# A transformer block on one core: the second LayerNorm's result modulated by ScalarE's copy, the router's moments taken on TensorE, b1's order from one mask, and the last steps in another order

## The chip, the cores and the metric

The kernel runs on one core of one Trainium2 chip. A core has five engines that work side by side, each on its own queue of instructions: PE (TensorE, matmuls), DVE (VectorE), ACT (ScalarE), POOL (GpSimd) and SP (SyncE, here only DMA issues). The metric is the device time of one execution in microseconds (us); less is better. A change of more than 2% is called faster or slower.

## The reference

Eight sequences of 256 tokens with 128 features go through causal attention with 16 heads of 8 and through a mixture of eight experts, both under adaptive LayerNorm:

```python
mod = (_silu(L0_c) @ L0_wmod).reshape(8, 6, 1, -1)
sa, ca, ga, sb, cb, gb = (mod[:, i] for i in range(6))   # ga, gb: magnitude at least 0.25
h = _layernorm(x) * (1 + ca) + sa
x = x + ga * attention(h, W_qkv, W_o)        # causal, ALiBi slopes
h = _layernorm(x) * (1 + cb) + sb
x = x + gb * ffn(h, W1, b1, W2, b2, ln_gamma, ln_beta, Wr, br)

# ffn: its input goes to the experts as it is; the router sees a LayerNorm of it
hr = (h - mu) * rsqrt(var + 1e-5) * ln_gamma + ln_beta
probs = softmax(hr @ Wr + br)                # 8 experts
# expert 0 has W1, b1, W2, b2; experts 1 to 7 all have the same perturbed copies
out = sum_e probs[e] * (gelu(h @ W1[e] + b1[e]) @ W2[e] + b2[e])
# perturbed copy: w * 0.2 for the largest 5% of |w|, w * 1.8 for the smallest 5%
```

Since experts 1 to 7 are equal, the kernel computes two experts and weighs the second with the sum of seven probabilities. The thresholds of the perturbation are found for W1 and W2 by a search over 31 bits, and for the short vectors b1 and b2 by rank: for each element, how many are larger and how many are smaller.

## The kernel before, in words

The order of every engine's instructions is written out by hand. After a prologue comes a loop over steps `t` = 0 to 39 on all engines, four steps per batch (`G` = 4 groups of 4 heads), and after it a last stage that is written line by line.

In step `t`, `s_unit` makes scores whose maxima DVE takes (L1204, L1208, into `nmax`); five steps later `e_unit` makes the same scores again with the maxima subtracted, ACT takes the exponential (L584, into `PT`), POOL applies the causal mask (L494), and `pv` (L819, L824) multiplies with the values. `ut` (L837) transposes the result `U`, which ACT has copied out (L694); after every second group DVE normalizes it into `A` (`rden` L1415, `A` L1419). At offset `AT_OT` = 10 of a batch `A` is transposed (L1020) and copied (`AT`, L590), at `AT_Y` = 11 it is projected with the gated output weight (L1027), and DVE adds it to `x_all` (L1425). Through step 31 each step also carries a bit of the threshold search: ACT and DVE count over `wa` (L599, L1183), PE sums the counts (`total`, L930, L932), DVE decides.

Then the second half of the block begins for that batch. `second_stats` (DVE, L1227, L1230) takes its moments, `second_rstd` (POOL, L437, L439) the inverse deviation, `second_normal` (POOL, L451) writes `n2`. `second_use` (DVE, L1239, two instructions) multiplies `n2` by 1 + cb and adds sb, with rows that DMAs have broadcast to all partitions (`rows_bc`), into `h2`. `router_stats` (DVE, L1249, L1252) takes the moments of `h2` for the router's LayerNorm. For each pair of batches `p`, `c_pe_h` (PE, L858) transposes `h2`, `c_act_h` (ACT, L607) copies it out as `h2T`, and `c_pe_l` (PE, L865) multiplies it with `wrg` (Wr scaled by gamma) for the logits. `router_logits` (DVE, L1261 to L1270), `c_exp` (POOL, L460, a power of e) and `router_weights` (DVE, L1275 to L1287) make the weights of the two experts. `f1(n)` and `f2(n)` (PE, L898 and L918) are the two layers of pair `n // 2`, of expert 0 for even and of the perturbed expert for odd `n`; `f1_ahead` (L881) does the first layer for `n` = 0 and 2 in steps 26 to 34. `combine(n)` (DVE, L1302; for odd `n` also L1309, L1315) adds the result of `f2(n)`.

`psX`, the last bank of PSUM, serves many in turn. Whoever writes to it next calls `claim_x(reader)`: PE first waits until the last reader named has read, and the queue behind it on PE waits too.

For b1's ranks POOL makes eight masks (`bias_masks`, L475, one in each of steps 8, 9, 12, 13, 16, 17, 18 and 20: b1 larger and b1 smaller than a column of 128 of its elements, four columns), PE sums them with a vector of ones (L1052, in steps 21 to 26), and DVE makes the perturbed b1 in step 27 (`perturb_b1`, L1335 to L1339). For b2 the masks are made by DVE in step 23 (L1354), summed in step 31 (L1044), and used in step 32. `find_tiers` and `perturb` (L1324 to L1331) do the same for W1 in steps 33 and 34, and for W2 in steps 38 and 39.

Of the kernel before, what the change touches and what calls it, by code (L numbers as in the profile page):

```python
# [23 lines left out]
P = 128  # L24
# [4 lines left out]
NC = FF // P  # L29
# [21 lines left out]
SIGNS_STEP, VEC_STEP, ROWS_STEP, SIZE_STEP, BIAS_STEP, WO_STEP = 0, 0, 1, 7, 31, 7  # L51
ROW_DMAS = 4
# [3 lines left out]
AT_STAT2, AT_STAT3 = AT_Y, AT_Y + 3  # L56
# [3 lines left out]
H2_AT = {AT_Y + G * b + 2 + (b >= LATE): b for b in range(B - 1)}  # L60
RSTD3_AT = {22: 0, 30: 1, 38: 2}
# [15 lines left out]
POOL_SETS = 9  # L77
# [8 lines left out]
def adaln_block(nc, x, w_qkv, w_o, w1, b1, w2, b2, gamma, beta, wr, br, c, wmod,  # L86
                k_const, q_const, ident_c, parts_dram, rows_dram, thr_dram, out):
    with ExitStack() as ctx:
# [3 lines left out]
        def sem(name):  # L92
# [26 lines left out]
        wrg = sb("wrg", [P, NE])  # L119
# [6 lines left out]
        rows_bc = sb("rows_bc", [P, B, 4, D])  # L126
# [30 lines left out]
        n2 = sb("n2", [P, 4, D])  # L157
        h2 = sb("h2", [P, NPAIR, 4, D])
        h2T = sb("h2T", [P, 2, 4 * P])
        mv3 = sb("mv3", [P, B * NBLK, 2])  # L160
        ve3 = sb("ve3", [P, B * NBLK])
        rs3 = sb("rs3", [P, B * NBLK])
        lgT = sb("lgT", [NE, 4 * P])
# [13 lines left out]
        rmask = hid.rearrange("p a c t -> p (a c t)").bitcast(BF16).rearrange("p (m k c t) -> p m k c t", m=2, k=2, c=NC)[:, 1]  # L177
# [8 lines left out]
        rows = lgT.rearrange("e (r d) -> e r d", r=4)  # L186
# [13 lines left out]
                 "ln_stat", "ln_rstd", "neg_mean", "n1_done", "t_done", "h1_done", "qk_done", "v_done", "v_out",  # L200
# [4 lines left out]
                 "tot_done", "cond_done", "ln2_stat", "ln2_rstd", "n2_done", "h2_done", "gate_in", "ln3_stat", "ln3_rstd",  # L205
# [6 lines left out]
        rows_in = [sem(f"rows_in{i}") for i in range(ROW_DMAS)]  # L212
# [36 lines left out]
        def _(sp):  # L249
# [11 lines left out]
            block_in(1)  # L261
            sp.dma_start(wa[0:HALF, :], w1.rearrange("(p r) f -> p (r f)", r=2)).then_inc(q["wa_in"], 16)
# [14 lines left out]
            def rows_to_dram():  # L277

                sp.wait_ge(q["dve_set"], SETS["rows"])
                sp.wait_ge(q["act_set"], ACT_SETS["cg"])  # L280
                sp.dma_start(rows_dram, rows[:, :, :]).then_inc(q["rows_out"], 16)
# [5 lines left out]
            def other_rows(i):  # L287
                bs = slice(i * B // ROW_DMAS, (i + 1) * B // ROW_DMAS)
                for b in range(bs.start, bs.stop):
                    sp.dma_start(rows_bc[:, b, 1:4, :], rows_dram[b, 1:4, :].partition_broadcast(P)).then_inc(rows_in[i], 16)  # L290
# [60 lines left out]
            other_rows(0)  # L351
# [6 lines left out]
            other_rows(1)  # L358
            sp.dma_start(w1_sb[:, :], w1).then_inc(q["w1_in"], 16)
            sp.dma_start(w2_sb[:, :, :], w2.rearrange("(c p) d -> p c d", p=P)).then_inc(q["w2_in"], 16)  # L360
            for b in range(4, B):
# [3 lines left out]
                if b < 6:  # L365
                    other_rows(b - 2)
# [17 lines left out]
        def _(gp):  # L384
# [4 lines left out]
            for i in range(3):  # L389
                gp.memset(Vx[:, i], 1.0).then_inc(q["pool_set"], 1)  # L390
            gp.memset(beta_w[:, :], 1.0).then_inc(q["pool_set"], 1)

# [32 lines left out]
            def gate(b):  # L425

                if b == 0:
                    gp.wait_ge(q["pe_set"], 7)
# [15 lines left out]
            def second_normal(b):  # L444

                gp.wait_ge(q["ln2_rstd"], b + 1)
                if b >= 2:
                    gp.wait_ge(q["h2_done"], b - 1)
                for i in range(NBLK):
                    k = NBLK * b + i  # L450
                    last = gp.tensor_scalar(n2[:, NBLK * (b % 2) + i, :], x_all[:, b, i, :], mv1[:, k, 0:1], rs1[:, k:k + 1],  # L451
# [3 lines left out]
            def router_ln(p):  # L455
                deviation("ln3_stat", (2 * p, 2 * p + 1), ve3, mv3, rs3, "ln3_rstd")
# [1061 lines left out]
```

## Time and profile before

| | us |
|---|---|
| median of 3 runs | 238.66 |
| the three runs | 238.48, 238.66, 248.0 |
| the profiled execution's own time | 239.84 |
| its span in the trace | 238.1 |

The profiled execution is a run of its own, with 239.84 us of which the trace covers 238.1; the 1.7 us around it lie before the first and after the last instruction. Times in the trace are counted from the start of the span. In the trace's windows, steps 0 to 31 run from about 18 to 158 us, steps 32 to 39 to about 185 us, and the last stage to the end.

### The profile page before, as it was taken

To read this page: it belongs to the slowest core of one execution; us is meant where nothing else is said; L and a number is where in the kernel's file an instruction comes from. 1 tells how busy PE (TensorE), PEld (TensorE's weight loads), DVE (VectorE), ACT (ScalarE), POOL (GpSimd) and SP (SyncE) were. 2 spreads that over 40 slices of the span, in tenths; PEclk is the share of its full clock that TensorE was granted. 3 is DMA by queue.
4 is the path that set the end of the run, shared out by engine and by line. 5 is a ranking of instruction groups with operands and counts; after the bars stand their busy time and mean duration, and the time that the engine had idled before them with its cause. 6 is when DMAs were issued, how large, how long until landed. Compare 5 with 4: busy or idle time off the path is not lost.

```text
span 238.1 us, 5477 instructions
## 1 busy us (share of the span) xinstructions
PE 216.5 (91%) x1901; PEld 152.5 (64%) x1918; DVE 185.0 (78%) x562; ACT 162.6 (68%) x344; POOL 143.6 (60%) x223
## 2 busy tenths in 40 slices
PE   8977989899899899889879879979879999999993
PEld 3554757676676676666667556735535878766793
DVE  4767899889799899998998876974967585675464
ACT  2577658989989989979669769937628741453320
POOL 8650232758979979988666236437779608283600
PEclk9997999999999999999999999999985999999999
DMA  6668665965948137237036000000000001010011
GB/s 179 118 185 224 153 168 140 243 183 143 249 120 211 41 95 213 53 96 194 6 89 181 26 0 6 0 0 6 3 0 3 0 3 44 0 45 3 0 44 44
DMA packets 19461, 20.90 MB, mean 88 GB/s; under 512 B 1547, under 2 KB 17562, under 8 KB 18370
## 3 DMA queue, kind: packets, MB, share of 16 engines
q1 hardware_dynamic: 18746, 20.22, 32.5%
q10 hardware_dynamic: 688, 0.33, 0.5%
q8 instruction: 15, 0.25, 0.4%
q14 instruction: 12, 0.10, 0.2%
HBM read 15.16 MB, written 5.26 MB: 86 GB/s over the span
## 4 chain that ended last, share of the span: by engine, by line
PE 63%; DVE 18%; ACT 7%; issue 7%; POOL 4%; ACTq 0%; DVEq 0%; POOLq 0%
PE bank L918 12%; PE bank L898 10%; PE bank L819 6%; DVE nmax L1208 4%; PE bank L715 4%; PE bank L776 4%; ACT msk L599 3%; PE bank L798 3%; PE bank L881 3%; PE bank L772 3%; PE bank L952 3%; PE bank L824 2%; DVE msk L1183 2%; PE bank L932 2%; PE bank L930 2%
## 5 line engine op out<-in xcount | busy, mean ns | idle before, releaser
L494 POOL TENSOR_SCALAR_AFFINE_SELECT PT<-PT 128x256 f32<-128x256 f32 (+1 forms) x96 | 46.8, 502 | 35.0 <-ACT PT L584 32.8
L599 ACT ACTIVATE msk<-wa,cand 128x1024 bf16<-128x1024 f32 (+1 forms) x62 | 57.7, 941 | 5.3 <-DVE cand L1194 5.3
L584 ACT ACTIVATE PT<-bank 128x512 f32<-128x512 f32 x96 | 55.5, 607 | 5.0 <-PE bank L793 3.4
L1208 DVE TENSOR_REDUCE nmax<-bank 128x2 f32<-128x512 f32 x64 | 43.5, 685 | 2.5 <-PE bank L776 1.8
L460 POOL TENSOR_TENSOR ex<-eul,lg 128x32 f32<-128x32 f32 x4 | 21.7, 5436 | 17.2 <-DVE lg L1270 17.2
L1204 DVE TENSOR_REDUCE nmax<-bank 128x4 f32<-128x512 f32 x32 | 21.7, 677 | 4.3 <-PE bank L769 4.2
L776 PE MATMUL bank<-Ks,Qs 78*128 78x256 bf16 x128 | 24.8, 276 | 0.0
L798 PE MATMUL bank<-Qs,Ks 80*128 80x256 bf16 x128 | 24.5, 273 | 0.2 <-ACT PT L584 0.2
L1183 DVE TENSOR_SCALAR_CACHE_REDUCE msk<-wa,cand 128x512 bf16<-128x512 f32 x31 | 23.1, 746 | 1.1
L819 PE MATMUL bank<-PT,Vx 128*32 128x256 f32 x256 | 20.9, 398 | 1.6 <-POOL PT L494 1.0
L772 PE MATMUL bank<-mask 128*128 128x256 bf16 x64 | 18.0, 281 | 2.9 <-DVE nmax L1208 2.4
L694 ACT ACTIVATE U<-bank 128x256 f32<-128x256 f32 x32 | 12.7, 398 | 11.5 <-PE bank L824 11.4
L624 ACT ACTIVATE hid<-bank,b1p 128x512 f32<-128x512 f32 x16 | 10.7, 687 | 10.6 <-PE bank L898 10.6
L1302 DVE SCALAR_TENSOR_TENSOR yt<-bank,pr,yt 128x128 f32<-128x128 f32 x32 | 9.1, 345 | 10.6 <-PE bank L918 10.5
L715 PE MATMUL bank<-ones_b 128*128 128x512 bf16 x49 | 16.3, 454 | 1.0 <-POOL ones_b L385 1.0
L898 PE MATMUL bank<-h2T,w1p 128*128 128x512 f32 x32 | 16.8, 656 | 0.0
L918 PEld LDWEIGHTS bank<-w2p,hid 128*128 128x128 f32 x128 | 14.8, 192 | 1.4 <-issue 1.4
L837 PE MATMUL bank<-ident,U 128*128 128x128 f32 x64 | 13.4, 292 | 1.7 <-DVE A L1419 1.0
L918 PE MATMUL bank<-w2p,hid 128*128 128x128 f32 x128 | 14.9, 275 | 0.0
L769 PE MATMUL bank<-Ks,Qs 78*128 78x128 bf16 x128 | 12.4, 218 | 1.9 <-DMA Ks<-parts 0.9
L776 PEld LDWEIGHTS bank<-Ks,Qs 78*128 78x128 bf16 x128 | 12.8, 100 | 1.8 <-issue 0.3
L769 PEld LDWEIGHTS bank<-Ks,Qs 78*128 78x128 bf16 x128 | 9.9, 97 | 5.8 <-issue 1.3
(196 smaller groups left out, 489.6 us busy)
## 6 DMA issues: line engine op xcount, KB each, us to landing
Qs<-parts SPq DMA_DIRECT2D x7, 576.0 KB
Ks<-parts SPq DMA_DIRECT2D x7, 576.0 KB
parts<-part SPq DMA_DIRECT2D x7, 384.0 KB, 2.8
rows_bc<-rows_out SPq DMA_DIRECT2D x8, 192.0 KB, 7.9
x_all<-in_x SPq DMA_DIRECT2D x8, 128.0 KB, 7.0
parts<-part SPq DMA_DIRECT2D x8, 128.0 KB, 2.9
out<-ob SPq DMA_DIRECT2D x3, 256.0 KB, 2.3
wa<-in_w SPq DMA_DIRECT2D x2, 256.0 KB, 4.6
```

What stands on the lines that cost most here:

```text
L494: gp.affine_select(out=v, in_=v, compare_op=ALU.is_ge, fill=0.0, base=0, pattern=[[0, v.shape[1]], [1, P]], channel_multiplier=-1).then_in ...
L584: act.activation(PT[:, e % 2, j], psE[u % 2][:, :], ACT.Exp).then_inc(q["exp_done"], 1)
L599: act.activation(scratch, wa[:, 0:width], ACT.Sign, bias=cand[:, col:col + 1].bitcast(F32), scale=-(1.0 - 2.0 ** -24), accum_out=acc[:, co ...
L715: mm(psU.rearrange("p (a k) -> p a k", a=HG), ones_b[:, :], ones4, start=True, stop=True)
L772: mm(bank.rearrange("p (h k) -> p h k", h=2)[:, :, P:S], mask5[:, HG, :], mask5[:, 0:2, :], start=True, stop=False, skip_group_check=True)
L776: last = mm(bank[:, i * S:(i + 1) * S], Qs[0:R_S, r, h, P:S], Ks[0:R_S, r, h, :], start=False, stop=True, skip_group_check=True)
L798: last = mm(bank[:, i * S:(i + 1) * S], Ks[0:R_E, r, h, 0:P], Qs[0:R_E, r, h, :], start=True, stop=True, skip_group_check=True)
L819: mm(psO[32 * i:32 * i + 32, 0:S], Vx[:, b % 4, 0, h, :], PT[:, e % 2, 1 + i // 2, (i % 2) * S:(i % 2 + 1) * S], start=True, stop=False, s ...
L898: mm(psF[ch][:, :], wt[:, ch * P:(ch + 1) * P], h2T[:, p % 2], start=True, stop=True).then_inc(q["f1_done"], 1)
L918: last = mm(bank[:, i * P:(i + 1) * P], hid_of(n)[:, ch, i * P:(i + 1) * P], wt[:, ch, :], start=(ch == 0), stop=(ch == NC - 1), skip_grou ...
L1183: ve.tensor_scalar(msk[:, 3], wa[:, ON_ACT:2 * FF], cand[:, BOT:BOT + 1].bitcast(F32), 0.0, op0=ALU.is_le, op1=ALU.add, accum_out=acc_d[:, ...
L1208: ve.tensor_reduce(nmax[:, b % 2, 1, h:h + 2], bank.rearrange("p (h k) -> p h k", h=2), axis=AX.X, op=ALU.max, negate=True).then_inc(q["ma ...
```

## The change

The second modulation (1 + cb, sb) leaves DVE and the DMAs: `n2` itself is transposed, so that a feature is a partition, and ACT's copy out of PSUM multiplies and adds with one column per batch (`mod2T`), in two instructions of half the size. `second_use`, `router_stats` and the broadcasts of the two modulation rows go; of the four rows per batch only ga's and gb's are still broadcast, gb's by one DMA behind the loads of batch 7. `mod2T` comes from two small matmuls in the prologue.

The router's moments now come from PE: `wrg` has a ninth column with 1/128, so that the logits' matmul yields the mean too; DVE squares `h2T` (`squares`), and four more matmuls yield the mean of the squares.

```diff
             def c_pe_l(p):
-                pe.wait_ge(q["h2T_done"], p + 1)
+                pe.wait_ge(q["h2T_done"], 2 * (p + 1))
                 claim_x((q["lg_read"], p + 1))
                 for i in range(4):
-                    last = mm(psX[:, i * NE:(i + 1) * NE], h2T[:, p % 2, i * P:(i + 1) * P], wrg[:, :], start=True, stop=True)
+                    last = mm(psX[:, i * (NE + 1):(i + 1) * (NE + 1)], h2T[:, p % 2, i * P:(i + 1) * P], wrg[:, :], start=True, stop=True)
                 last.then_inc(q["lg_psum"], 1)
+                pe.wait_ge(q["sq_done"], p + 1)
+                for i in range(4):
+                    last = mm(psX[:, MSQ_COLS + i:MSQ_COLS + i + 1], sq[:, i * P:(i + 1) * P], wrg[:, NE:NE + 1], start=True, stop=True)
+                last.then_inc(q["sq_sum"], 1)
...
+            def squares(p):
+                v.wait_ge(q["h2T_done"], 2 * (p + 1))
+                if p:
+                    v.wait_ge(q["sq_sum"], p)
+                ve.tensor_tensor(sq[:, :], h2T[:, p % 2], h2T[:, p % 2], op=ALU.mult).then_inc(q["sq_done"], 1)
...
+            def router_moments(p):
+                raw = psX[:, 0:4 * (NE + 1)].rearrange("p (i e) -> p i e", i=4)
+                v.wait_ge(q["sq_sum"], p + 1)
+                then_self(ve.tensor_copy(mean3[:, :], raw[:, :, NE]))
+                ve.tensor_tensor(msq3[:, :], mean3[:, :], mean3[:, :], op=ALU.mult)
+                then_self(ve.tensor_tensor(lt[:, :, :], e8(mean3[:, :]), g8(gsum[:, 0:NE]), op=ALU.mult))
+                ve.scalar_tensor_tensor(ve3[:, 4 * p:4 * p + 4], psX[:, MSQ_COLS:MSQ_COLS + 4], EPS, msq3[:, :], op0=ALU.add,
+                                        op1=ALU.subtract).then_inc(q["ln3_var"], 1)
+                ve.tensor_tensor(lg[:, :, :], raw[:, :, 0:NE], lt[:, :, :], op=ALU.subtract).then_inc(q["lg_read"], 1)
...
                 combine(n)
                 p = n // 2 + 1
-                if p < NPAIR:
-                    (router_weights if n % 2 else router_logits)(p)
+                if p < NPAIR and n % 2 == 0:
+                    squares(p)
+                    router_moments(p)
+                    router_logits(p)
+                elif p < NPAIR:
+                    router_weights(p)
```

For pair 0 the squares are made in step 32, `c_pe_l(0)` stands at the end of step 33 (before: step 36), the moments in step 34.

For b1 there is one mask per column instead of two: DVE makes all four at the end of step 31, and the instruction's own accumulator gives the count of larger elements the other way; PE sums them at the end of step 32 (16 matmuls instead of 32), `perturb_b1` stands in step 33. b2's masks are made in step 7.

```diff
-B1_AT, B1_USE = (8, 9, 12, 13, 16, 17, 18, 20), 27
-B1_RANKS = {21: (0,), 22: (1,), 23: (2, 3), 24: (4,), 25: (5,), 26: (6, 7)}
...
+            def bias_masks():
+                v.wait_ge(q["b1abs_done"], 1)
+                for i in range(NC):
+                    last = ve.tensor_scalar(rmask[:, i], b1a[:, :], colsa[:, i:i + 1], 0.0, op0=ALU.is_gt, op1=ALU.add,
+                                            accum_out=b1_over[:, i:i + 1])
+                last.then_inc(q["b1m_done"], 1)
...
+                if t == BIAS_STEP + 1:
+                    pe.wait_ge(q["b1m_done"], 1)
+                    claim_x((q["b1p_done"], 1))
```

The remaining edits move work. In the prologue `w_o` is loaded by SP instead of ACT's queue and its transpose follows `projected(0)`, with one spare matmul ahead of that instead of two; the variance plus epsilon of batch 0 is made by DVE; in step 0 the second scores and two spare matmuls stand ahead of `total`. In steps 36 to 39 the four parts of `f1(1)` stand ahead of `ut` instead of at the end of the step, and in step 32 `f1_ahead` stands ahead of `pv`. DVE adds to `x_all` ahead of `rden` and `A`. POOL's `router_ln` takes its variance from `router_moments`.

On PE, the start of the last stage of before (w_sb are the plain weights, w2p and w1p the perturbed ones):

```order
L1027 MATMUL bank<-woTg,AT 128x128 x2
L898 MATMUL bank<-h2T,w1p 128x512
L918 MATMUL bank<-w_sb,Qs 128x128 x16
L865 MATMUL bank<-wrg,h2T 128x8 x4
L898 MATMUL bank<-h2T,w1p 128x512 x4
L918 MATMUL bank<-w2p,hid 128x128 x16
```

and the same place of the changed kernel:

```order
L891 MATMUL bank<-h2T,w1p 128x512
L1032 MATMUL bank<-woTg,AT 128x128 x2
L911 MATMUL bank<-w_sb,Qs 128x128 x16
L854 MATMUL bank<-wrg,h2T 128x9 x4
L858 MATMUL bank<-wrg,sq 128x1 x4
L891 MATMUL bank<-h2T,w1p 128x512 x4
L911 MATMUL bank<-w2p,hid 128x128 x16
```

The four matmuls on `sq` are new, between the logits of pair 1 and `f1(3)`; the same stands twice more, for pairs 2 and 3.

On DVE, from `x_all` of batch 5 (step 31) to the first part of `find_tiers` of W1 (step 33), before:

```order
L1425 TENSOR_TENSOR x_all<-x_all,bank 128x256
L1227 BN_STATS st<-x_all 128x6 x2
L1230 BN_AGGR mv<-st 128x2 x2
L1389 COPY Ks<-bank 128x512
L1335 TENSOR_SCALAR b2t<-bank 128x128
...
L1389 COPY Ks<-bank 128x512
L1415 RECIPROCAL rden<-bank 128x16
L1419 TENSOR_TENSOR A<-bank,rden 128x2x64
L1097 TENSOR_SCALAR w1p<-w_sb 128x512
```

and in the changed kernel:

```order
L1416 TENSOR_TENSOR x_all<-x_all,bank 128x256
...
L1226 BN_STATS st<-x_all 128x6 x2
L1229 BN_AGGR mv<-st 128x2 x2
L1343 TENSOR_SCALAR hid,b1_over<-b_bc,colsa 128x512 x4
L1391 COPY Ks<-bank 128x512
L1327 TENSOR_SCALAR b2t<-bank 128x128
...
L1237 TENSOR_TENSOR sq<-h2T 128x512
L1391 COPY Ks<-bank 128x512
L1327 TENSOR_SCALAR rtmp<-b1_over 128x4
...
L1422 RECIPROCAL rden<-bank 128x16
L1426 TENSOR_TENSOR A<-bank,rden 128x2x64
L1097 TENSOR_SCALAR w1p<-w_sb 128x512
```

The four masks (L1343), the squares (L1237) and the five instructions of the perturbed b1 (from L1327 on) have come in.

## Rows read from the trace of the kernel before

**Rows 1.** The page: each engine's busy time, and TensorE's granted clock in 40 slices.

```profile
PE 216.5 (91%) x1901; PEld 152.5 (64%) x1918; DVE 185.0 (78%) x562; ACT 162.6 (68%) x344; POOL 143.6 (60%) x223
PEclk9997999999999999999999999999985999999999
```

**Rows 2.** Busy time of each engine by window (start:end, length, busy us, clock).

```profile
62.00:97.00 35.00, 32.60 (x358) 23.36 (x361) 32.30 (x97) 32.48 (x74) 31.59 (x55) 1.00 0.56 151
97.00:132.00 35.00, 31.37 (x372) 23.01 (x375) 31.67 (x89) 29.70 (x68) 25.54 (x43) 1.00 0.38 101
157.90:174.40 16.50, 13.77 (x145) 7.71 (x145) 12.34 (x31) 10.28 (x22) 10.64 (x19) 1.00 0.01 3
185.00:200.00 15.00, 15.00 (x114) 13.09 (x113) 10.61 (x36) 7.07 (x12) 7.56 (x6) 1.00 0.00 1
```

**Rows 3.** The chain that ended last, last stage (start, length, what).

```profile
189.28 3.54 PE bank L898 x8
192.82 3.57 PE bank L918 x32
...
200.40 0.79 PE bank L865 x8
```

**Rows 4.** Groups of instructions by line and shape (busy us, mean ns).

```profile
L475 POOL TENSOR_SCALAR hid<-b_bc,colsa 128x512 bf16<-128x512 f32 x8 | 12.6, 1574 | 0.0
L1239 DVE TENSOR_TENSOR h<-n,rows_bc 128x256 f32<-128x256 f32 x8 | 3.9, 483 | 2.3 <-POOL n L451 2.3
L1239 DVE TENSOR_TENSOR h<-h,rows_bc 128x256 f32<-128x256 f32 x8 | 3.6, 446 | 0.3
L1249 DVE BATCH_NORM_STATS2 st<-h 128x6 f32<-128x128 f32 x16 | 3.8, 282 | 0.1
L541 ACT ACTIVATE h1T<-bank,modT 128x256 f32<-128x256 f32 x8 | 4.5, 564 | 4.3 <-PE bank L942 4.3
L1052 PE MATMUL bank<-ones_b,hid 128*128 128x1 bf16 x32 | 1.6, 163 | 2.6 <-DVE x_all L1425 1.3 <-ACT AT L590 1.3
L1183 DVE TENSOR_SCALAR_CACHE_REDUCE msk<-wa,cand 128x512 bf16<-128x512 f32 x31 | 23.1, 746 | 1.1
L439 POOL TENSOR_TENSOR rs<-ve,mhalf 128x4 f32<-128x4 f32 x4 | 4.2, 1040 | 0.3
L1267 DVE TENSOR_TENSOR lg<-lg,rs 128x32 f32<-128x32 f32 x4 | 0.8, 192 | 0.1
```

**Rows 5.** The chain that ended last, steps 13 and 14.

```profile
72.37 1.56 POOL hid L475
...
78.83 0.92 POOL hid L475
```

**Rows 6.** Waits: who waited for whom, total, times, longest.

```profile
PE bank L1027 <- DVE b1p L1339: 1.2, 1, 1.2
```

**Rows 7.** Prologue: two spare matmuls ahead of the first projection; the window at 20 us.

```profile
7.00 1.06 PE L715 MATMUL bank<-ones_b 128*128 128x512 bf16 x2
20.00:21.00 1.00, 1.00 (x5) 0.39 (x4) 0.86 (x3) 0.97 (x3) 0.00 (x0) 0.50 0.94 274
```

**Rows 8.** Instructions in order of time, steps 31 to 37.

```profile
157.93 0.41 DVE L1425 TENSOR_TENSOR x_all<-x_all,bank 128x256 f32<-128x256 f32 x1
...
174.41 0.41 DVE L1425 TENSOR_TENSOR x_all<-x_all,bank 128x256 f32<-128x256 f32 x1
174.64 0.41 PE L837 MATMUL bank<-ident,U 128*128 128x128 f32 x2 [1.00 <-DVE A L1419]
...
178.46 5.44 POOL L460 TENSOR_TENSOR ex<-eul,lg 128x32 f32<-128x32 f32 x1
```

**Rows 9.** Instructions of DVE in order of time, last stage.

```profile
193.42 1.12 DVE L1302 SCALAR_TENSOR_TENSOR yt<-bank,pr,yt 128x128 f32<-128x128 f32 x4
...
201.46 0.19 DVE L1275 TENSOR_REDUCE esum<-ex 128x4 f32<-128x32 f32 x1 [2.38 <-POOL ex L460]
...
203.58 0.69 DVE L1287 TENSOR_TENSOR yt<-yt 128x512 f32<-128x512 f32 x1
```

More of the change, by code:

```diff
@@ L285, in gate_rows, with last_rows @@
                 sp.dma_start(rows_bc[:, :, 0, :], rows_dram[:, 0, :].partition_broadcast(P)).then_inc(q["gate_in"], 16)
[L287 to L290, printed above, removed]
+            def last_rows():
+                sp.dma_start(rows_bc[:, :, 1, :], rows_dram[:, 1, :].partition_broadcast(P)).then_inc(q["gb_in"], 16)
             def write_first():
@@ L606, in c_act_h @@
                     act.wait_ge(q["lg_psum"], p - 1)
-                act.activation(h2T[:, p % 2], (psE[1] if p >= 2 else psQ)[:, :], ACT.Copy).then_inc(q["h2T_done"], 1)
+                    act.wait_ge(q["sq_done"], p - 1)
+                for k in range(2):
+                    b = 2 * p + k
+                    act.activation(h2T[:, p % 2, S * k:S * (k + 1)], (psE[1] if p >= 2 else psQ)[:, S * k:S * (k + 1)], ACT.Identity,
+                                   scale=mod2T[:, 1, b:b + 1], bias=mod2T[:, 0, b:b + 1]).then_inc(q["h2T_done"], 1)
             def gelus(n, chunks=range(NC)):
@@ L974, in _ @@
             mm(psE[1][0:B, 0:512], c_s[:, :], wmod_sb[:, 2 * D:6 * D], start=True, stop=True).then_inc(q["pe_set"], 1)
+            pe.wait_ge(q["dve_set"], SETS["modT"])
+            for j in range(2):
+                last = mm(psE[0][:, j * B:(j + 1) * B], wmod_sb[:, (3 + j) * D:(4 + j) * D], c_s[:, :], start=True, stop=True)
+            last.then_inc(q["pe_set"], 1)
             turned(1)
@@ L1004, in _ @@
                     total(n)
+                if first and t in AHEAD and t >= B * G:
+                    f1_ahead(*AHEAD[t])
                 pv(t)
@@ L1011, in _ @@
                 e_unit(t, 2)
-                if t in AHEAD and t >= B * G:
+                if t in AHEAD and t >= B * G and not first:
                     f1_ahead(*AHEAD[t])
+                if t in F1_STEPS:
+                    f1(1, F1_STEPS[t])
                 ut(t)
@@ L1039, in _ @@
                     router_sums()
+                if t == BIAS_STEP + 1:
+                    pe.wait_ge(q["b1m_done"], 1)
+                    claim_x((q["b1p_done"], 1))
+                    for m in range(NC):
+                        for j in range(NC):
+                            last = mm(psX[:, B1_COLS + m:B1_COLS + m + 1], rmask[:, j, m * P:(m + 1) * P], ones_b[:, 0:1],
+                                      start=(j == 0), stop=(j == NC - 1), skip_group_check=True)
+                    last.then_inc(q["b1rank"], 1)
+                if t in H_STEP:
+                    c_pe_h(H_STEP.index(t))
+                if t in AHEAD and t < B * G:
+                    f1_ahead(*AHEAD[t])
                 if t == BIAS_STEP:
@@ L1429, in _ @@
                     second_stats(b)
-                if t in H2_AT:
-                    second_use(H2_AT[t])
-                b = batch_at(t, AT_STAT3)
-                if b is not None:
-                    router_stats(b)
                 if t == SIGNS_STEP:
@@ L1455, in _ @@
                     perturb_b2()
-            second_use(B - 1)
-            router_stats(B - 1)
+                if t == SQUARE_STEP:
+                    squares(0)
+                if t == MOMENT_STEP:
+                    router_moments(0)
             router_weights(0)
```

204 lines of the change are left out of this document (81 added, 123 removed).

## The prediction

> **What bounds the kernel now.** I read the page first. TensorE is busy for 216.5 of 238.1 us, the others for 60 to 78% [rows 1]; but a busy share is an average, so the stages are read one by one. The windows of the loop [rows 2] show that no engine rules there: from 62 to 132 us (70 us) ACT is busy for 32.48 + 29.70 = 62.2 us, DVE for 64.0, PE for 64.0, POOL for 57.1. Whoever is late in a step holds up the next one, so work taken from one engine gives back only a part. In the last stage it is another picture: PE is busy for 15.00 of 15.00 us [rows 2], and the chain of waits there runs over PE alone, eight blocks of `f2` (3.57 us) and five of `f1` (3.54) with the logits' 0.79 between [rows 3]. DVE has slack there, but what PE waits for in that stage moves the end one for one. Between the two, in steps 31 to 39, DVE is busy for 12.34 of 16.50 us [rows 2], and its chain decides when PE may go on (1.00 us of waiting for `A` at 174.64) [rows 8]. Clock: TensorE's granted clock is at its full level (2.4 GHz) but for two dips to half of it (1.2 GHz), in slice 4 and in slices 30 and 31 of the page [rows 1].
>
> **The change part by part. Loop.** DVE loses `second_use` and `router_stats`: 3.9 + 3.6 + 3.8 = 11.3 us over eight batches [rows 4], 1.4 each and some small aggregates, four of them in the 70 us. POOL loses eight masks, 12.6 us [rows 4], in steps 8 to 20; two of them stand on the chain for 1.56 + 0.92 = 2.5 us [rows 5]. PE loses 16 of 32 rank matmuls, and two places where its whole queue stood behind them: 1.3 us behind `x_all` [rows 4], 1.2 us behind the perturbed b1 [rows 6]. If the 70 us shrank to what PE and ACT have to do (62.4, with 0.8 us less on PE and a bit of cleared waiting), 7.6 would be won. Today 6 of 70 us are lost although three engines are close to full; with DVE relieved I leave 4 of them, so 66.3 and a gain of 3.7. With b1's 1.2, which lies behind 132 us, the loop gives 4.9. Bounds: 2.5 (only the stretch on POOL's chain) and 9.5 (7.6, b1's wait, and the same rate for the steps to 158 us).
>
> **Prologue.** One of two spare matmuls ahead of the first projection goes: half of 1.06 us at most [rows 7], I take 0.4. Putting the second scores of step 0 ahead of `total` fills PE's wait there. At 20 us the clock was at half [rows 7]; if it stays up, 1 to 2 us of PE's time are saved, of which DVE, busy for 0.86 us in that window, lets through about half: 1.0. The DMA of `w_o`, now in SP's queue ahead of `wa`, can take some of it back. Together 1.4, bounds 0 and 2.4. The two small matmuls for `mod2T` stand beside PE's wait for ACT; ACT's two copies replace two others.
>
> **Steps 31 to 37.** DVE gets four masks, 4 x 0.746 less their overlap = 2.8 us (the same instruction, a compare with an accumulator over 512 columns, is the threshold count) [rows 4]; `squares(0)`, 0.69 as any two-input instruction of 128x512 [rows 9]; five small instructions for b1, about 1.0; the moments, five at 0.19 [rows 4], 0.95. It loses one `second_use` and `router_stats`, about 2.2 here. Net 3.3: from 12.34 to 15.6 of 16.5 us [rows 2]. That would just fit if it never waited, but now it does. At the end of step 32 PE must claim `psX` behind `perturb_b2`, which on DVE has moved behind the masks (2.8 us later), and in step 34 the transpose of `A` claims the same bank behind `router_moments(0)`, which stands behind `find_tiers` and `perturb`. I followed both queues from `x_all` of batch 5 (157.93 us): the moments end at 174.2, PE then does step 35 (1.9 us) and the projection, and `x_all` of batch 6 ends at 177.0 instead of 174.41 + 0.41 = 174.8 [rows 8]. So +2.2 us; bounds 0 and +4. Moving `f1(1)` ahead of `ut` saves PE some 4 us up to `f2(0)`, but the next paragraph shows why nobody gets them.
>
> **Last stage.** Behind `f2(0)` PE does the logits of pair 1 and now waits for `squares(1)`, which DVE does after `combine(0)`, which waits for `router_weights(0)`, which waits for POOL's power for pair 0. Before, that power ended at 178.46 + 5.44 = 183.90, 9.1 us after `x_all` of batch 6 [rows 8], and nobody on PE cared. Now: 177.0 + 9.1 = 186.1; router weights 203.58 + 0.69 - 201.46 = 2.8 [rows 9]; `combine` 1.12 [rows 9] and `squares` 0.69, with gaps 1.85; four more matmuls, which cost what the logits' four cost, 0.79 [rows 3]. `f1(3)` starts at 191.65 instead of 189.28 [rows 3]: +2.4, which holds the +2.2 above.
> From there to `f1(4)` it took 201.19 - 189.28 = 11.9 us [rows 3]. Now, from the start of `f1(3)`: moments 0.95, the inverse deviation 1.04 [rows 4] (before it was long done), logits 0.9, power 5.44, all with gaps: 8.4. `combine(1)` begins at 3.54 + 3.57 = 7.1 and takes 2.65, `router_weights(1)` to 12.6, `combine(2)` and `squares(2)` to 14.5, the four matmuls to 15.3. +3.4. For pair 3 the same sum gives 17.1 against 15.3: there PE has one `f1` more in between and only its own wait counts. +1.8. The sum of the stage is 2.4 + 3.4 + 1.8 = 7.6 us. The least it can cost is one time 1.85 per pair (the wait for `combine` and `squares`, of which the logits hide 0.79, and 0.79 for the new matmuls): 5.6, if DVE is never late. ACT's copy `h2T` in two instructions costs 2 x 0.564 [rows 4], some 0.5 us more per pair, beside a whole `f2`.
>
> **Sum.** 7.6 - 4.9 - 1.4 = +1.3 us on the span of 238.1 and on the profiled execution's 239.84. The median of the runs is 238.66, 1.2 us under that execution, so 238.66 + 1.3 = 240.0 us.
>
> **Rivals.** *The stalls bring the clock down.* In each of the three places PE now does 0.79 us of matmuls of 9 columns, stands still for 1 to 2.6 us and does 0.79 us with one column. The two dips of before came behind the same picture: the second began about 2 us after PE had waited 1.00 us for `A` at 174.64 [rows 8], with the logits of pair 0 in between, and covers some 6.5 us of slices 30 and 31 [rows 1]. In 6.5 us at half the clock 3.3 us are lost. It decides from the point where the first stall is answered by a clock of 0.5 in `f1(3)`: one dip gives 243.3, three give 249.9. For it: the picture. Against it: PE waited 1.3 us at one blow in the loop [rows 4], and no dip followed. The Trainium skill, TensorE: Matmul & The Clock Gate, Part 1, says that the rate follows how busy the array was lately and has just these two levels, which is this rival; the rows agree that it falls behind poorly filled stretches, and do not tell whether these are poor enough. Chance 0.22.
> *The removed work was not on the chain.* DVE's modulation does not appear in the chain of waits of the loop; if only POOL's 2.5 us come back and the prologue gives nothing, 238.66 + 7.6 - 2.5 = 243.8. Chance 0.17.
> *The loop gives much more.* 9.5 and 2.4 from the upper bounds, and steps 31 to 37 cost nothing: 5.6 - 11.9 = -6.3, 232.4. For it: with three engines near full, relief of two may loosen more than I leave. Chance 0.16.
> My forecast holds 0.45.
>
> **The numbers.** 2% of 238.66 is 4.8 us, about what a measurement here can tell from no change; so faster is below 233.9, slower above 243.4. Faster: most of the third rival (0.11) and a tail of the forecast (0.03), 0.14. Slower: of the clock's what is more than one dip (0.14), half of the second's (0.09), and a tail of the forecast (0.05), 0.28. Same: 0.58. The range reaches from 234.0 (into the third rival) to 247.0 (one or two dips).
>
> **What would show it.** In the changed kernel's chain of waits: three stalls of PE between the two groups of small matmuls, ended by DVE's `sq`, 2 to 3 us from the end of each `f2` to the next `f1`; a distance from the start of `f1(3)` to `f1(4)` of 15.3 us. In step 34 a PE wait before the transpose of `A` that DVE's `lg` ends. Steps of the loop (spacing of the first `nmax`) shorter by 0.1 to 0.2 us from step 8 on. A clock of 1.0 at 20 us. If the loop shrinks by over 8 us, or if `squares` is ready before PE asks, the forecast is too high; a half clock in the last stage makes it too low.

## The result and the profile after

The changed kernel takes 250.24 us (median of four runs, 247.39 to 251.96), the kernel before 239.13 us in the runs beside it: ratio 1.043, 95% interval 1.031 to 1.055. It is 11 us slower, where +1.3 was forecast, and lies outside the range. In a later round on another chip, the same file gave 250.21 us and 1.042 (1.035 to 1.048). Single executions of a kernel can take some per cent longer at a lower granted clock and are left out of the ratios; the profiled execution of the changed kernel (251.96 us, 1.7 us over its median) is one of these, so what is read from it is set beside other traces further down.

The page of the changed kernel, busy times and two lines of its slices:

```profile
span 250.2 us, 5459 instructions
...
PE 224.8 (90%) x1922; PEld 159.1 (64%) x1938; DVE 177.3 (71%) x539; ACT 163.8 (65%) x348; POOL 129.5 (52%) x211
...
PE   7779989899999999999999999699985987998993
...
PEclk9995999999999999999999999657998897999999
```

Against before [rows 1], DVE is busy for 7.7 us less, POOL for 14.1 less, ACT for about as long (163.8 us against 162.6), and PE for longer (224.8 against 216.5). The clock line says why: there is half clock in slice 4, in 26 to 28, in 31 and 32, and in 34. Places in the two traces, set against each other, say what each stretch cost. The stretches are cut at `x_all` of batches 5 and 6 and at the starts of `f1` as the chain of waits has them (192.04 us for `f1`(3), 0.14 us behind the start in the timeline below):

| stretch | before | after | difference | predicted |
|---|---|---|---|---|
| start to step 1 (first `nmax`) | 24.34 | 25.87 | +1.5 | -1.4 |
| step 1 to `x_all`(5) | 133.59 | 126.72 | -6.9 | -4.9 |
| `x_all`(5) to `x_all`(6) | 16.48 | 22.81 | +6.3 | +2.2 |
| `x_all`(6) to `f1`(3) | 14.87 | 16.64 | +1.8 | +0.2 |
| `f1`(3) to `f1`(4) | 11.91 | 17.28 | +5.4 | +3.4 |
| `f1`(4) to `f1`(6) | 15.3 | 19.32 | +4.0 | +1.8 |
| `f1`(6) to the end | 21.6 | 21.6 | 0 | 0 |
| sum | | | +12.1 | +1.3 |

The sum is that of the spans, 250.2 against 238.1.

The timeline of PE after, behind step 31 (start, duration, line, operation; in brackets PE's idle time ahead of it and who ended it):

```profile
155.86 0.39 PE L787 MATMUL bank<-Qs,Ks 80*128 80x256 bf16 x2
156.43 0.44 PE L826 MATMUL bank<-ident,U 128*128 128x128 f32 x2 [0.18 <-ACT U L683]
159.06 0.56 PE L1051 MATMUL bank<-ones_b,hid 128*128 128x1 bf16 x16 [2.19 <-DVE b2p_bc L1331]
...
170.47 1.84 PE L874 MATMUL bank<-h2T,w_sb 128*128 128x512 f32 x2
172.14 0.38 PE L826 MATMUL bank<-ident,U 128*128 128x128 f32 x2
172.36 0.38 PE L1025 MATMUL bank<-ident,A 128*128 128x128 f32 x2
```

And in the last stage:

```profile
187.43 0.96 PE L854 MATMUL bank<-wrg,h2T 128*128 128x9 f32 x8
190.99 1.05 PE L858 MATMUL bank<-wrg,sq 128*128 128x1 f32 x8 [2.60 <-DVE sq L1237]
191.90 5.38 PE L891 MATMUL bank<-h2T,w1p 128*128 128x512 f32 x8
...
208.27 1.05 PE L858 MATMUL bank<-wrg,sq 128*128 128x1 f32 x8 [2.61 <-DVE sq L1237]
209.18 5.38 PE L891 MATMUL bank<-h2T,w_sb 128*128 128x512 f32 x8
...
227.59 1.05 PE L858 MATMUL bank<-wrg,sq 128*128 128x1 f32 x8 [1.22 <-DVE sq L1237]
228.50 3.68 PE L891 MATMUL bank<-h2T,w_sb 128*128 128x512 f32 x8
```

The windows of the same stretches (busy time of each engine, then the granted clock, DMA share and GB/s):

```profile
157.00:159.00 2.00, 0.00 (x0) 0.00 (x0) 1.86 (x7) 0.00 (x0) 1.30 (x3) 0.86 0.00 0
159.00:172.00 13.00, 12.94 (x86) 8.24 (x87) 7.66 (x21) 4.14 (x8) 4.69 (x8) 0.50 0.01 2
190.00:192.00 2.00, 1.01 (x9) 1.01 (x10) 0.90 (x2) 0.00 (x0) 0.00 (x0) 1.00 0.00 0
192.00:196.00 4.00, 4.00 (x7) 1.72 (x7) 1.45 (x9) 1.37 (x2) 2.13 (x2) 0.57 0.00 0
209.00:213.00 4.00, 4.00 (x8) 1.81 (x9) 1.45 (x9) 1.15 (x2) 1.86 (x2) 0.58 0.00 0
```

Read them together. PE stands still for 2.19 us at the end of step 32 because DVE has not finished b2; from the last 0.6 us of that wait on it has half its clock (1.2 GHz), for 13.6 us in all, and from 159 to 172 us it is busy for 12.94 of 13.00 us. `f1`(3) and `f1`(4), each behind a wait of 2.6 us for the squares, show 5.38 us for eight rows that take 3.68 at `f1`(6), behind a wait of only 1.22. The forecast's own rows are all there: the three waits ended by `sq`, in the right places. What was not there is the wait ahead of `A`'s transpose in step 34 (172.36): at half clock PE comes to that place later than DVE.

One correction to the section on the change: b2's masks and the absolute values of b1 and b2 stand in step 30, not in step 7 (DVE makes the masks at 149.41). It changes no term of the sum.

### The profile page after: what moved, and what is told of

Same layout as the page of the kernel before. It is cut to its first block, busy times and chain, and to the rows that moved or that the text cites. A ratio compares the mean times of both kernels' runs of the same rounds, so it can differ in the third digit from the quotient of the medians.

```text
span 250.2 us, 5459 instructions
## 1 busy us (share of the span) xinstructions
PE 224.8 (90%) x1922; PEld 159.1 (64%) x1938; DVE 177.3 (71%) x539; ACT 163.8 (65%) x348; POOL 129.5 (52%) x211
## 4 chain that ended last, share of the span: by engine, by line
PE 55%; DVE 23%; issue 5%; ACT 5%; DMA 5%; POOL 3%; SPq 1%; DVEq 0%; ACTq 0%
PE bank L911 9%; PE bank L891 8%; PE bank L808 5%; DVE nmax L1207 5%; PE bank L765 3%; PE bank L787 3%; DVE msk L1182 3%; PE bank L874 3%; PE bank L761 3%; PE bank L704 2%; PE bank L923 2%; POOL ex L453 2%; PE bank L813 2%; DMA wa<-in_w 2%; PE bank L945 2%
## 5 line engine op out<-in xcount | busy, mean ns | idle before, releaser
L787 PE MATMUL bank<-Qs,Ks 80*128 80x256 bf16 x128 | 25.5, 281 | 0.6 <-ACT PT L569 0.6
L1203 DVE TENSOR_REDUCE nmax<-bank 128x4 f32<-128x512 f32 x32 | 21.6, 676 | 5.1 <-PE bank L758 5.1
L449 POOL TENSOR_TENSOR rs<-ve,mhalf 128x4 f32<-128x4 f32 x4 | 4.1, 1020 | 24.7 <-DVE ve L1249 24.7
L613 ACT ACTIVATE hid<-bank,cols 128x512 f32<-128x512 f32 x8 | 5.5, 687 | 17.1 <-PE bank L891 17.1
L761 PEld LDWEIGHTS bank<-mask 128*128 128x128 bf16 x64 | 7.7, 120 | 10.3 <-DVE nmax L1207 6.4
```

What stands on the lines that cost most here:

```text
L761: mm(bank.rearrange("p (h k) -> p h k", h=2)[:, :, P:S], mask5[:, HG, :], mask5[:, 0:2, :], start=True, stop=False, skip_group_check=True)
L787: last = mm(bank[:, i * S:(i + 1) * S], Ks[0:R_E, r, h, 0:P], Qs[0:R_E, r, h, :], start=True, stop=True, skip_group_check=True)
```

## The experiments

Theory C (clock): the long waits for DVE are the cause, but most of the loss comes from the clock that falls behind them. Rival W (waits alone): the waits and the new matmuls themselves cost the time. Theory M: DVE's four masks in step 31 make the wait of step 32. Theory P: the prologue's edit costs time. Theories C and M, with the wait as the cause and the clock behind it, can both hold. Runs of different groups ran on different chips, so their ratios to the kernel before are what is compared.

**First group.** The changed kernel once more:

> The changed kernel itself, on the same chip as the three edits sent with it, so that they can be set against it. All theories: about 250 us, 1.04 times the kernel before, a PE wait of about 2.2 us ahead of b1's rank matmuls in step 32 and half clock behind it until about 172 us, and PE waits of 2.6, 2.6 and 1.2 us for the squares in the last stage.

Measured: 250.21 us, ratio 1.042 (1.035 to 1.048).

*Spare matmuls in the waits*, in `c_pe_l` and in step 32 (`fill(bank, k)` makes k matmuls of 512 columns that nobody reads):

```diff
                 last.then_inc(q["lg_psum"], 1)
+                if p:
+                    fill(psE[1], 12)
                 pe.wait_ge(q["sq_done"], p + 1)
...
                     pe.wait_ge(q["b1m_done"], 1)
+                    pe.wait_ge(q["max_done"], 3 * G * B)
+                    fill(psS[1], 10)
                     claim_x((q["b1p_done"], 1))
```

> The changed kernel plus spare matmuls (nothing reads them) in the four places where PE waits for DVE: 10 ahead of b1's rank matmuls in step 32, 12 between the logits and the squares' sums of pairs 1, 2 and 3. The waits for DVE stay as long as they are, only PE isn't idle in them. Clock theory (the idle stretches themselves cost little, the granted clock that falls behind them costs about 3.7 us in steps 32 to 34 and 1.7 us each at f1(3) and f1(4)): 7 us faster than the changed kernel, about 243 us, granted clock 1.0 from 155 us on. Waits-alone theory (the extra time is the waits and the added small matmuls, the clock is only beside it): no faster than the changed kernel, 250 to 252 us, since nothing is taken from the path and pair 3's 12 spare matmuls overrun its wait by about 1.3 us.

Measured: 244.28 us, 1.022 (1.016 to 1.027). Work that nobody reads made the kernel 6 us faster than it was on the same chip (250.21); C holds and W alone falls. Its clock line, whose one low digit is slice 4:

```profile
PEclk9997999999999999999999999999999999999999
```

PE's timeline at the same place as above:

```profile
181.33 0.96 PE L858 MATMUL bank<-wrg,h2T 128*128 128x9 f32 x8
182.14 2.75 PE L708 MATMUL bank<-ones_b 128*128 128x512 bf16 x12
184.88 1.05 PE L864 MATMUL bank<-wrg,sq 128*128 128x1 f32 x8
185.79 3.68 PE L897 MATMUL bank<-h2T,w1p 128*128 128x512 f32 x8
```

`f1`(3) follows the logits' end as late as before, yet takes 3.68 us. This run also prices the waits without the clock: `x_all`(5) to `x_all`(6) 18.60 us (150.70 to 169.30), against 22.81, so 4.2 us of that stretch were clock; `f1`(3) to `f1`(4) 15.59, against 17.28, 1.7 us. Pair 3's spare matmuls overrun their wait: `f1`(4) to `f1`(6) is 18.74 us (201.38 to 220.12), where the changed kernel's 19.32 less the 1.70 us of half clock in `f1`(4) is 17.6. These 1.1 us are about what the result lies above the expected 243.

*b1's ranks in a bank of their own.*

```diff
                 elif ch < 3:
                     pe.wait_ge(q["max_done"], 3 * G * B)
+                    if ch == 2:
+                        pe.wait_ge(q["b1p_done"], 1)
...
-                    claim_x((q["b1p_done"], 1))
+                    pe.wait_ge(q["max_done"], 3 * G * B)
...
-                            last = mm(psX[:, B1_COLS + m:B1_COLS + m + 1], rmask[:, j, m * P:(m + 1) * P], ones_b[:, 0:1],
+                            last = mm(psS[1][:, m:m + 1], rmask[:, j, m * P:(m + 1) * P], ones_b[:, 0:1],
```

The first of these edits is in `f1_ahead`: its third part writes to the bank that the ranks now use, and so has to wait until DVE has read them.

> The changed kernel with b1's ranks in a PSUM bank of their own (the one of the score maxima, free by then), so that they needn't wait for DVE's b2 arithmetic: the wait of 2.2 us in step 32 has no reason left, the last stage is as it was. Clock theory: 2.2 us of wait and about 3.7 us of half clock go, 244 to 245 us, clock 1.0 through steps 32 to 34. Waits-alone theory: 2.2 us go, about 248 us. A third possibility, that the half clock there has another cause (the 16 one-column rank matmuls): it stays low behind them, and about 2 us go.

Measured: 252.55 us, 1.056 (1.050 to 1.061), slower than the changed kernel: a miss of all three. PE's timeline of it:

```profile
154.26 0.55 PE L1053 MATMUL bank<-ones_b,hid 128*128 128x1 bf16 x16
...
156.00 0.39 PE L787 MATMUL bank<-Qs,Ks 80*128 80x256 bf16 x2
...
159.09 1.74 PE L876 MATMUL bank<-h2T,w_sb 128*128 128x512 f32 x2 [2.70 <-DVE b1p L1333]
```

The rank matmuls don't wait any more, and the clock is 1.00 on them and until 158 us: these 16 matmuls of one column didn't bring it down. But the score bank that they now use is needed by the next `f1_ahead`, which waits for the perturbed b1, and that lies 2.3 us further down DVE's queue than b2 (done at 158.9 us, b2 at 156.6). The wait was moved and got longer (2.70 us), and the half clock came with it. `x_all`(5) to `x_all`(6) is 22.50 us (149.99 to 172.49), against 22.81: nothing is gained there. That the kernel got slower still comes from the last stage, whose code is unchanged. There the square sums ahead of `f1`(3) take 1.86 us instead of 1.05, and `f1`(6) is at half clock too, a third dip:

```profile
226.56 5.38 PE L893 MATMUL bank<-h2T,w_sb 128*128 128x512 f32 x8
```

So giving the ranks another bank doesn't help as long as DVE's queue is what they wait for, which points to theory M.

*The squares earlier.*

```diff
+            squares(1)
             router_weights(0)
             for n in range(2 * NPAIR):
+                if n == 4:
+                    squares(3)
                 combine(n)
                 p = n // 2 + 1
+                if n == 1:
+                    squares(2)
                 if p < NPAIR and n % 2 == 0:
-                    squares(p)
```

> The changed kernel with DVE's squares of pairs 1, 2 and 3 ahead of router_weights(0), router_weights(1) and combine(4), so that PE's square sums follow its logits at once. Step 32 stays. Clock theory: 2.6 + 2.6 + 1.2 us of waits and 2 x 1.7 us of half clock in f1(3) and f1(4) go, 9.8 us, about 240.5 us. Waits-alone theory: 6.4 us, about 244 us. If the squares push combine or router_weights back by their 0.7 us each and PE then waits there: 242 to 243 us.

Measured: 239.65 us, 0.996 (0.991 to 1.001): 10.6 us less than the changed kernel on the same chip, where C expected 9.8 and W 6.4. The clock line:

```profile
PEclk9955699999999999999999999985599999999999
```

PE's timeline:

```profile
191.08 0.96 PE L854 MATMUL bank<-wrg,h2T 128*128 128x9 f32 x8
191.89 1.03 PE L858 MATMUL bank<-wrg,sq 128*128 128x1 f32 x8
192.78 3.68 PE L891 MATMUL bank<-h2T,w1p 128*128 128x512 f32 x8
...
203.88 0.96 PE L854 MATMUL bank<-wrg,h2T 128*128 128x9 f32 x8
```

1.9 us of small matmuls in a row, but no wait: no dip in the last stage. The dip of step 32 (slices 27 to 29) is still there, and so is its wait (2.20 us). The one in slices 3 to 5 is taken up at the end. `f1`(3) to `f1`(4) is 12.81 us (192.78 to 205.59), 0.9 over the kernel before; that is the price of the four new matmuls, for which 0.79 was counted.

**Second group.** *The masks one per step*, with the absolute values of b1 and b2 in step 26:

```diff
-                if t == BIAS_STEP:
-                    bias_masks()
+                if 0 <= t - 27 < NC:
+                    bias_mask(t - 27)
```

> The changed kernel with b1's four masks one each in steps 27 to 30 (the absolutes in step 26) instead of all four in step 31, so that DVE's b2 arithmetic comes 2.7 us earlier and PE's claim of psX in step 32 finds it done. The last stage is as it was. Theory: DVE's backlog of masks makes the stall in step 32, and the stall the half clock. Stall and half clock go (2.2 + 3.7 us); the masks cost in the loop what DVE isn't waiting for there, 0 to 2.7 us: 244 to 247 us. Rival, the half clock in steps 32 to 34 comes from the rank and router matmuls with few columns: it stays, 248 to 250 us.

Measured: 245.45 us, 1.022 (1.017 to 1.027). M holds: neither the wait of step 32 nor the half clock behind it (slices 26 to 30) is there any more. The rank and router matmuls are the same ones, so the rival that matmuls with few columns bring the clock down there falls:

```profile
PEclk9999999999999999999999999999997997997998
```

DVE's addition to `x_all` of batches 5 and 6 in its timeline:

```profile
149.98 0.41 DVE L1417 TENSOR_TENSOR x_all<-x_all,bank 128x256 f32<-128x256 f32 x1
...
166.24 0.42 DVE L1417 TENSOR_TENSOR x_all<-x_all,bank 128x256 f32<-128x256 f32 x1 [2.55 <-PE bank L1032]
```

And PE's timeline between them:

```profile
163.15 0.44 PE L1025 MATMUL bank<-ident,A 128*128 128x128 f32 x2 [1.52 <-DVE lg L1251]
```

16.26 us, less than the kernel before needed (16.48), and now, with PE on time, the wait ahead of `A`'s transpose appears that the forecast named. (`f1`(6) has a third dip here too.) In the loop the four masks cost nothing: 126.8 us from step 1 (23.16) to `x_all`(5), as without them.

*Both together, and six spare matmuls ahead of step 0.*

> masks_spread and the early squares together: no PE stall for DVE in step 32 nor behind f2(0), f2(2), f2(4). Theory: gains add, 239.7 (early squares alone) less 3 to 6 us: 234 to 237 us, clock 1.0 from step 2 to the end, and thus faster than the kernel before by 1 to 2%. Rival, the two gains overlap since both only move the same chain (POOL's power for pair 0): 238 to 239 us.

> combo2 plus six spare matmuls ahead of step 0, in PE's wait of 1.3 us for the DMA of the stacked parts. Theory: the half clock at 19 to 25 us comes behind that wait, as in step 32; with the wait filled it stays away and step 1 begins at 23.2 us in every execution: 1 to 2 us faster than combo2, and with less spread. Rival, DMA alone sets the first steps: as combo2.

```diff
             total(1)
             values(1)
+            spare(6)
```

Measured: 235.37 us, 0.977 (0.972 to 0.982), and with the spare matmuls 232.89 us, 0.970 (0.966 to 0.974). The gains add: 4.6% from the early squares and 1.9% from the spread masks would make 0.977 out of 1.042. Only the second version is clearly more than 2% faster than the kernel before. Its clock line:

```profile
PEclk9999999999999999999999999999999999999999
```

What the spare matmuls give is less sure, since the two intervals overlap: the profiled execution of the version without them has half clock from 11.3 us on, ahead of the place where they stand (17.2 us). They cannot have kept that one away.

*The prologue's loads and PE's order up to `values(0)` as before* (the order of step 0 stays changed):

```diff
-            sp.dma_start(wo_in[:, :], w_o).then_inc(q["wo_in"], 16)
+            act.dma_start(wo_in[:, :], w_o).then_inc(q["wo_in"], 16)
...
-            spare(1)
-            projected(0)
             pe.wait_ge(q["wo_in"], 16)
             tr(psO[:, 0:P], wo_in[:, :], ident[:, :]).then_inc(q["pe_set"], 1)
-            spare(4)
+            spare(2)
+            projected(0)
+            spare(5)
```

> The changed kernel with the prologue's DMA of w_o and PE's order up to values(0) as before (w_o on ACT's queue, its transpose ahead of the projection, two and five spare matmuls). Theory (the prologue's change gives about 1 us when the clock stays up, and the profiled execution lost it to a dip that had nothing to do with it): 250 to 251.5 us, up to 1 us slower than the changed kernel. Rival (the DMA of w_o in SP's queue ahead of wa delays the first copies and with them the first scores): 1 to 2 us faster, 248.5 to 249.5 us.

Measured: 250.90 us, 1.046 (1.041 to 1.050), against 1.042 (1.035 to 1.048) with the edit in: P, which wanted a gain of 1 to 2 us, finds no support, and the medians can't tell the two apart. Step 1 in the traces: 25.87 us in the changed kernel, whose clock is at half from 18.5 to 25.3 us, but 23.20 and 23.16 with the bank of its own and with the masks spread, whose code is the same up to there and whose clock stays up; before 24.34, with a dip of 3.4 us. With the edit taken back and the clock at 1.00 all the way it is

```profile
25.11 0.67 DVE L1203 TENSOR_REDUCE nmax<-bank 128x4 f32<-128x512 f32 x1
```

so at full clock the edit brings step 1 forward by 1.9 us, one trace against two.

This execution (249.85 us) also checks the table above, since behind the prologue its code is that of the changed kernel: `x_all`(5) to `x_all`(6) is 21.73 us (151.58 to 173.31), and from there to `f1`(3), `f1`(4), `f1`(6) and the end 16.63, 17.28, 19.32 and 21.6. The three dips behind step 30 are all there, the first with 10.2 us instead of 13.6.

**Third group.** *One wait put back into the fastest version.*

```diff
-            squares(1)
             router_weights(0)
...
-                if n == 1:
-                    squares(2)
+                if n < 2:
+                    squares(n + 1)
```

> combo3 (masks spread, squares early, spare matmuls ahead of step 0: 232.9 us, clock 1.0 throughout) with one thing put back: the squares of pair 1 behind combine(0), as in the changed kernel. In combo3's trace combine(0) ends at 180.85 and PE has its logits done at 178.9, so PE waits for about 2.0 us. Clock theory: the wait and 1.8 us of half clock in f1(3) behind it, 232.9 + 3.8 = 236.7 us. Waits-alone theory: 232.9 + 2.0 = 234.9 us.

Measured: 238.89 us, 1.001 (0.998 to 1.005) against 0.970: 6.0 us by the medians and 7.5 by the ratios for one wait, more than either theory gave. PE's timeline:

```profile
178.35 0.96 PE L854 MATMUL bank<-wrg,h2T 128*128 128x9 f32 x8
181.91 1.87 PE L858 MATMUL bank<-wrg,sq 128*128 128x1 f32 x8 [2.60 <-DVE sq L1238]
183.64 5.67 PE L891 MATMUL bank<-h2T,w1p 128*128 128x512 f32 x8
...
196.72 0.96 PE L854 MATMUL bank<-wrg,h2T 128*128 128x9 f32 x8
```

The wait is 2.60 us where I had worked out 2.0; the square sums take 1.87 instead of 1.03 and `f1`(3) 5.67 instead of 3.68, 2.8 us of clock, and the spans differ by 5.9 (236.4 against 230.5). This is the cleanest price of one wait: itself, and about the same again. It is not a fixed price. Behind the same 2.60 us the changed kernel lost 1.7 us at `f1`(3); here the clock fell a microsecond before the wait ended, and the square sums ran at half clock too.

*GpSimd's and DVE's former load put back*, on scratch data, into the fastest version:

```diff
+                if t in (8, 9, 12, 13, 16, 17, 18, 20):
...
+                    gp.tensor_scalar(load[:, t % 4], wa[:, 0:FF], cols[:, 0:1], None, op0=ALU.is_gt)
...
+                    then_self(ve.tensor_tensor(ld[:, :], wa[:, FF:FF + 256], wa[:, FF:FF + 256], op=ALU.mult))
+                    then_self(ve.tensor_tensor(ld[:, :], ld[:, :], wa[:, FF:FF + 256], op=ALU.add))
...
+                        last = ve.bn_stats(ls[:, i, :], ld[:, i * D:(i + 1) * D])
```

DVE gets it for seven batches, 9.5 us of busy time (186.9 against 177.4).

> combo3 plus eight GpSimd compares of 128x512 (nothing reads them) in steps 8, 9, 12, 13, 16, 17, 18 and 20, where the kernel before had b1's masks: the load that the change took from GpSimd, put back alone. My split of the loop's gain of 6.0 us: about 2.5 us hung on GpSimd's masks, so 235.4 us. Rival, GpSimd's masks were covered: 232.9 us. Rival, most of the gain is theirs: 237 us or more.

> combo3 plus, for seven batches in the steps where the kernel before had them, two DVE operations of 128x256 and two statistics with their aggregates on scratch data: about the load that the change took from DVE, put back alone. If the loop's gain hung mostly on DVE: 3 us or more, 236 us. If DVE's work was off the chain: 0 to 1 us, 233 to 234 us.

> combo3 with both loads. If they add: the sum of the two, some 5 us, 238 us, which would account for the loop's gain but for b1's waits. If either covers the other, as three nearly full engines could: no more than the larger of the two. If they do more than their sum: work on both engines is what made the steps long.

Measured: 236.39 us (0.995, 0.991 to 0.999), 238.86 us (0.999, 0.995 to 1.004), 242.07 us (1.014, 1.009 to 1.020), against 0.970. The loop is read from step 1 to `x_all`(5). The latter in DVE's timeline of the fastest version:

```profile
149.79 0.41 DVE L1418 TENSOR_TENSOR x_all<-x_all,bank 128x256 f32<-128x256 f32 x1
```

With GpSimd's load:

```profile
153.97 0.41 DVE L1424 TENSOR_TENSOR x_all<-x_all,bank 128x256 f32<-128x256 f32 x1
```

With DVE's:

```profile
152.34 0.41 DVE L1421 TENSOR_TENSOR x_all<-x_all,bank 128x256 f32<-128x256 f32 x1
```

With both:

```profile
156.05 0.41 DVE L1427 TENSOR_TENSOR x_all<-x_all,bank 128x256 f32<-128x256 f32 x1
```

Less the starts of step 1 (23.24, 23.54, 24.07, 23.41): 126.55, 130.43, 128.27, 132.64 us. GpSimd's masks are worth 3.9 us, DVE's work 1.7, both together 6.1 of the 6.9 that the loop gained. They add, nearly (5.6). The spans rise by 4.1, 6.9 and 9.1 us; by the ratios it would be 6, 7 and 11, which the traces don't explain in full. For DVE's load the rise is larger than the loop's because PE waits longer for `lg` in step 34, and half clock follows again: `x_all`(5) to `x_all`(6) is 19.72 us (152.34 to 172.06), in the fastest version 16.25. From its waits (in total, times, longest):

```profile
PE bank L1029 <- DVE lg L1255: 3.0, 1, 3.0
```

From its windows:

```profile
164.00:166.00 2.00, 0.00 (x0) 0.00 (x0) 1.86 (x7) 0.00 (x0) 0.29 (x1) 1.00 0.00 0
...
168.00:170.00 2.00, 2.00 (x21) 0.75 (x19) 0.00 (x0) 1.19 (x3) 1.00 (x2) 0.50 0.00 0
```

## Why the prediction was wrong

**The step that failed** is the likeliest case itself: it priced every wait at its own length and left the clock where it was. The rival *The stalls bring the clock down* is what happened, and the sign that was named for it, half clock in the last stage, is in the trace. Its 249.9 for three dips is 0.3 us beside the median, but partly by luck: it placed all three dips in the last stage, where two came in the trace, had none in step 32, where the dearest one was, and priced each at 3.3 us, where 4.2, 1.7 and 1.7 came. The reason that I gave against it was that PE had waited 1.3 us in the loop without a dip. The row was right and the use of it wrong: it says nothing of waits of 2.2 to 2.6 us, and the rival itself spoke of standing still for 1 to 2.6 us. The clock's share in the trace: 4.2 us in steps 32 to 34 (changed kernel against spare matmuls; 3.1 in the trace with the prologue put back) and 1.7 each in `f1`(3) and `f1`(4), 7.6 us of the 10.8 that were missing. Another 2.7 us are the dip in the prologue (step 1 at 25.87 instead of 23.2), and the loop gave 2.0 more than forecast.

**Loop, -4.9.** Measured -6.9; inside the bounds. The split was off: I counted 2.5 us on GpSimd's chain, it is 3.9; of DVE's work 9.5 us, put back, cost 1.7. A small part of what DVE lost was thus on the chain, and the rival *not on the chain*, with 2.5 us for the whole loop, falls. The upper bound of 9.5 doesn't follow from its own parts, which make 11.6 (7.6 and 1.2, and 2.8 for the 26 us up to 158); nothing hung on it.

**Prologue, -1.4.** Measured +1.5. With the clock up, step 1 comes at 23.2 us, which is -1.1 and close; in the profiled execution the dip at 20 us came all the same and was longer. The term rested on a clock that the edit doesn't keep up, and the medians with and without the edit don't differ beyond their intervals.

**Steps 31 to 37, +2.2.** With the clock up, `x_all`(5) to `x_all`(6) is 18.60 us against 16.48: +2.1. Both queues were followed correctly. The claim in step 32 was known; what was missed is that PE stands still in it for 2.2 us and that the clock can fall there. Measured with it: +6.3.

**Last stage, 7.6 in all.** From `x_all`(6) to `f1`(3) 1.6 us were missing, and that is a mis-sized term. I took the 9.1 us from the end of `x_all`(6) to the end of pair 0's power from before [rows 8], but the change also moved pair 0's inverse deviation on GpSimd from step 30 to step 35, ahead of that power (first line; the second is the power):

```profile
175.37 1.04 POOL L449 TENSOR_TENSOR rs<-ve,mhalf 128x4 f32<-128x4 f32 x1
...
180.70 5.45 POOL L453 TENSOR_TENSOR ex<-eul,lg 128x32 f32<-128x32 f32 x1
```

The power ends 10.3 us behind the end of `x_all`(6), 1.2 us more than before; the other 0.4 lie between the power and `f1`(3), 5.9 us where 5.5 were counted. (The terms as they stand add up to 191.54, not 191.65.) `f1`(3) to `f1`(4) was forecast at 15.3 and is 15.59 with the clock up; `f1`(4) to `f1`(6) at 17.1 and is 19.32 less 1.70 of half clock (5.38 less the 3.68 that `f1`(4) takes with the early squares), 17.6. Those sums were right to half a microsecond, and so was the mechanism of the three waits, as the early squares show by taking it away.

**Sum without the clock.** Loop -6.9, prologue -1.1, steps 31 to 37 +2.1, last stage +1.8, +3.7 and +2.3: +1.9. By this sum from the traces the forecast of +1.3 would have been met if a waiting PE cost only the wait. The trace with spare matmuls bears it out: its span is 3.7 us over the kernel before, 1.1 of that is the overrun and 0.8 the dip in its prologue, which leaves +1.8. Its ratio of 1.022 (5.3 us) leaves about 4 us instead; the rest of these is open. The Trainium skill, TensorE: Matmul & The Clock Gate, Part 1, says that the throttled rate is the default and that activity releases it. The run with spare matmuls agrees: 1.022 against 1.042 for adding useless work.

## What to carry to other kernels

Where a wait for another engine is added to PE's path, price it twice: once as itself, once as the clock that may fall with it (here 1.7 to 4.2 us per wait), and count on the second part as soon as the wait is longer than any in the trace that the clock let pass. Before giving such a change up, look for what the awaited result is queued behind: here two moves on DVE, masks one per step and squares ahead of `router_weights` turned 4% slower into 2% faster. Giving a waiting matmul another bank doesn't help if the same queue must then free that bank. And a dip that moves between executions can hide or fake a gain of 1 or 2 us in a single trace.

## What the hardware showed that I had not expected

**Which waits the clock answered.** In the traces of eight versions every PE wait of 2.2 to 3.0 us behind step 30 came with half clock, 15 of 15; it began between 1.4 us before the end of the wait and 1.7 us behind it. None of the waits of 1.4 to 1.5 us in step 34 had it (six). Waits of 1.22 us behind small matmuls were followed by it in two traces of four. The dip of the kernel before began 2.2 us behind a wait of 1.00 us [rows 8]. The wait for the first scores was followed by it at 0.94, 0.98 and 1.29 us and not at 1.33. So the length of the wait alone doesn't decide below 1.5 us; what does isn't settled here.

**How long it stayed.** With the waits of 2.6 us in the last stage the half clock lasted 3.4 us seven times and 6.8 twice (one wait put back; bank of its own). With the 2.2 us of step 32 it lasted 13.6, 13.6 and 10.2 us, and in the first of these PE was busy for 12.94 of 13.00 us by its records; with the 2.7 us of the bank of its own 10.2; with the 3.0 us of step 34 (DVE's load and both loads) 6.8 and 3.4. So a longer wait didn't mean a longer dip. What decides the return isn't shown; the runs only show that where the wait is gone or filled, the dip is gone too.

**The first steps.** The clock up to 30 us differs between executions of the same code: step 1 starts at 23.2 us with it up, at 25.9 with one dip, and at 29.4 (early squares) where it was at half from 12 us on. Here too the low clock came with a longer wait. In the last of these PE had just waited 2.17 us for DVE, and 1.92 us in the first version with both changes, while in the other traces with this prologue the wait is 1.4 us at most and no dip begins right behind it:

```profile
11.43 0.71 PE L956 MATMUL bank<-wvT,h1T 128*128 128x128 f32 x4 [2.17 <-DVE resid L1153]
```

A term of 1 us in a prologue can't be read from one trace.
